# Attention stage: up products into the score ring, a DMA exchange for the rotary half, one exponential per quad, and the key's head mask on VectorE

## What is computed

```python
xn = layernorm(x)                                     # 32 sequences, T = 256, D = 128
q, k = l2norm(xn @ Wq), l2norm(xn @ Wk)               # 16 heads of 8
v = xn @ Wv
clock = softplus(xn @ clock_w + clock_b)              # one value per head
q, k = rope(q), rope(k)
gcp = exp(clip(cumsum(-softplus(xn @ gate_w + gate_b)), -60, 50))
q, k = q * gcp, k / (gcp + 1e-8)
p_exp = exp(p - max_t p) * clock                      # p = xn @ p_w + p_b
q, k = q / (cumsum(p_exp) + 1e-8), k * p_exp
out = softmax(causal(q @ k.T) / sqrt(8)) @ v
x1 = out @ out_w + out_b + residual
x2 = x1 + gelu(layernorm(x1) @ mlp_w1 + mlp_b1) @ mlp_w2 + mlp_b2
def rope(x): x1, x2 = even and odd elements of a head; return x1*cos - x2*sin, x1*sin + x2*cos
```

## Time and profile before

| | us |
|---|---|
| three runs, median | 2212.62 (2210.34 to 2213.51) |
| profiled execution, first to last instruction | 2164.4 |
| median less that span | 48.2 |
| one full step of the attention stage | 41.83 |
| full steps | 13 |
| first write of the expert layer's index table | about 769 |

### The profile page before, as it was taken

One profiled execution on the slowest core, in us unless ns is written; L12 is line 12 of the kernel. 1 busy time (PEld: TensorE's weight loads), 2 busy tenths in 40 slices (PEclk: granted clock), 3 DMA queues, 4 the chain that ended last, 5 costly groups with the idle time before them and its releaser, 6 DMA issues. The chain is left out here.

```text
span 2164.4 us, 37241 instructions
## 1 busy us (share of the span) xinstructions
PE 1849.2 (85%) x12576; PEld 954.5 (44%) x12600; DVE 1703.8 (79%) x3547; ACT 1474.7 (68%) x2917; POOL 1165.1 (54%) x720
## 2 busy tenths in 40 slices
PE   6999999999998459957889889898898988659996
PEld 2566666656665259952222222222222222124453
DVE  7778868877863437854899999999999998976776
ACT  5888888888885138845656666666666666437775
POOL 2122232242221027871789999999999998840001
PEclk9999999999999669977899999999999998879998
DMA  4100010011001012221100111001111100023333
GB/s 169 36 26 26 28 49 26 26 36 41 21 25 33 20 50 77 88 72 42 30 25 27 34 35 34 27 30 30 31 35 35 35 31 30 21 67 90 97 84 78
DMA packets 103708, 97.35 MB, mean 45 GB/s; under 512 B 9137, under 2 KB 86113, under 8 KB 103137
## 3 DMA queue, kind: packets, MB, share of 16 engines
q1 hardware_dynamic: 95584, 75.34, 12.4%
q0 software_dynamic: 6784, 18.10, 2.5%
q10 hardware_dynamic: 1152, 1.54, 0.2%
HBM read 45.87 MB, written 28.10 MB: 34 GB/s over the span
## 5 line engine op out<-in xcount | busy, mean ns | idle before, releaser
L1935 POOL TENSOR_TENSOR hc<-h,c_rep 128x1024 f32<-128x1024 f32 x256 | 627.8, 2463 | 137.9 <-DVE h L1899 136.7
L1899 DVE TENSOR_TENSOR_SCAN h<-decay,bank 128x1024 f32<-128x1024 f32 x241 | 551.0, 2286 | 22.5 <-issue 0.9
L1757 ACT ACTIVATE decay<-bank,neg_a_r 128x510 f32<-128x510 f32 x512 | 322.6, 683 | 257.5 <-PE bank L1634 257.1
L1618 PE MATMUL bank<-u_in,sel_rows 32*128 32x512 f32 x964 | 287.9, 675 | 95.7 <-DVE h L1899 95.6
L1634 PE MATMUL bank<-delta,sel_rows 32*128 32x512 f32 x1024 | 338.8, 677 | 0.9 <-ACT decay L1757 0.9
L1886 DVE TENSOR_TENSOR bank<-bank,b_rep 128x1024 f32<-128x1024 f32 x241 | 291.2, 1208 | 34.8 <-PE bank L1618 33.0
L992 POOL DMA_INDIRECT rows_in_dram<-row,idx x64 | 63.3, 989 | 318.3 <-DVE row L965 303.7
L574 ACT ACTIVATE es<-bank 128x384 f32<-128x384 f32 x512 | 208.9, 499 | 22.1 <-PE bank L373 21.8
L1618 PEld LDWEIGHTS bank<-u_in,sel_rows 32*128 32x128 f32 x964 | 76.0, 191 | 276.7 <-DVE h L1899 199.7
L1649 PE MATMUL bank<-hc,y_sel 128*32 128x512 f32 x1024 | 149.6, 660 | 0.8 <-POOL hc L1935 0.8
L1656 PE MATMUL bank<-xpad,w_conv 128*128 128x512 f32 x256 | 133.0, 634 | 3.2 <-ACT xc L1819 1.6
(11 more groups left out here) (341 smaller groups left out, 4170.0 us busy)
## 6 DMA issues: line engine op xcount, KB each, us to landing
r_tw<-r_o_t SPq DMA_DIRECT2D x96, 128.0 KB, 2.3
xvs<-xv SPq DMA_DIRECT2D x16, 512.0 KB, 2.9
u_wide<-u_rep_dram SPq DMA_DIRECT2D x30, 256.0 KB, 3.5
xs<-rows_in_dram SPq DMA_DIRECT2D x72, 68.0 KB, 1.8
front<-in_x_dram SPq DMA_DIRECT2D x16, 256.0 KB, 2.9
w<-in_w_dram SPq DMA_DIRECT2D x2, 2048.0 KB
xlb_dram<-front SPq DMA_DIRECT2D x16, 256.0 KB, 2.3
xlb_m<-xlb_dram SPq DMA_DIRECT2D x16, 256.0 KB
```

What stands on the lines that cost most here:

```text
L1618: last = pe.matmul(BD[n % 2][:, i * STEP:(i + 1) * STEP], sel[at:at + 32, r, :], u_in[p if n < NS else q][at:at + 32, hf, :], start=True, ...
L1757: act.activation(decay[n % 4][:, i, :, 1:], seq(DL[i])[:, :, 1:], ACT.Exp, scale=c["neg_a_r"][:, hf, g:g + 1]).then_inc(s["n_da"], 1)
L1899: dve.tensor_tensor_scan(flat(h[n % RING]), decay[n % 4].rearrange("p i b t -> p (i b t)"), flat(drive_0) if by_pool else BD[n % 2], 0.0, ...
L1935: pool.tensor_tensor(hc[n % RING][:, :, :], h[n % RING][:, :, :], c_rep[p if n < NS else q][:, :].unsqueeze(1).to_broadcast([P, 2, STEP]), ...
```

## The change

Five things change, all in the attention stage:

1. **Up products.** `up(0)` to `up(3)` write into the four banks of the ring, one after another, between `exps(5)` and `quad(6)`; the four gelus read them there. `quad(6)` waits for the last gelu. The down products are split: two token tiles ahead of `quad(7)`, two behind `weigh(6)`.
2. **Exchange.** The projections with `w_qs` and `w_ks` are gone. VectorE multiplies the one product with `cos` and with `sin`; two DMAs of 64 partitions each copy `rot_b` to `rot_s` with even and odd partitions exchanged (`swap`), and VectorE subtracts. That is four DMAs a step on SyncE's queue. The first product with `ones_blk` (L481) now waits for `rot_b` of q, and its place is ahead of `quad(0)`; the weights' load shrinks and is split in three.
3. **Merged exponentials.** `exps(n)` is one ScalarE instruction of 128x1536 over the four banks; `s_score` counts once a quad, at the last mask.
4. **The key's mask.** VectorE's last product with `pexp` is made four times, each with the mask as its scalar, at the start of the next step, between `pre[1]` and `pmax`; L953 and ScalarE's four copies are gone.
5. **Order.** On TensorE `back(3)` moves behind `quad(1)`, `weigh(7)` behind `quad(0)`, `quad(2)` ahead of `weigh(1)`, and the second product with `ones_blk` and the routing's product stand behind `back(0)`. On ScalarE `av_copy(3)` moves behind `exps(0)` and `exps(2)` ahead of `av_copy(0)`. GpSimd's L985 waits for `m_xl2` as well. `of` and `before` of the table's code move into `log`, to make room in SBUF.

```diff
+        def swap(sp, sem):
+            for to in range(2):
+                sp.dma_start(rot_s[to:P:2, :], rot_b[1 - to:P:2, :]).then_inc(sem, 16)
...
+                sp.wait_ge(s["f_rb"], one_on)
+                swap(sp, s["f_qsw"])
+                sp.wait_ge(s["f_kb"], one_on)
+                sp.wait_ge(s["f_rq"], one_on)
+                swap(sp, s["f_ksw"])
...
-                    pe.matmul(diag, c["ident_b"][:, :], c["mask_b"][:, :, :], start=False, stop=True,
-                              skip_group_check=True).then_inc(s["s_score"], 1)
+                    last = pe.matmul(diag, c["ident_b"][:, :], c["mask_b"][:, :, :], start=False, stop=True, skip_group_check=True)
+                last.then_inc(s["s_score"], 1)
...
             if tail:
                 pe.wait_ge(s["m_ht_sb"], k - 2)
-                up(0)
+                pe.wait_ge(s["s_exp"], 8 * (k - 2) + 6 if late else 8 * PAIRS)
+                for n in range(FC):
+                    up(n)
...
             if late:
+                if tail:
+                    pe.wait_ge(s["m_gelu"], 4 * k - 8)
                 quad(6, k - 2, p)
...
             if tail:
                 pe.wait_ge(s["m_gelu"], 4 * k - 8)
-                for j in range(TS):
...
+                down(range(0, 2))
             if late:
                 quad(7, k - 2, p)
-            if front:
-                pe.wait_ge(s["f_pe"], k + 1)
-                project(FB, c["w_qs"], s["f_qs"])
-            if late:
                 weigh(6, k - 2, p)
-                weigh(7, k - 2, p)
+            if tail:
+                down(range(2, TS))
+            if front:
+                pe.wait_ge(s["f_sq"], k + 1)
+                pe.wait_ge(s["f_rb"], k + 1)
+                pe.matmul(FA[:, :], c["ones_blk"], square[:, :], start=True, stop=True).then_inc(s["f_ssq"], 1)
...
             def exps(n, u):
-                for st in range(HS):
-                    act.wait_ge(s["s_score"], u * 32 + HS * n + st + 1)
-                    if st == 0:
-                        since(act, s["s_av"], u * 8 + n - 1)
-                    last = act.activation(es[(n % 2) * HS + st][:, :], RING[st][:, 0:3 * P], ACT.Exp, scale=DH ** -0.5)
-                last.then_inc(s["s_exp"], 1)
+                act.wait_ge(s["s_score"], u * 8 + n + 1)
+                since(act, s["s_av"], u * 8 + n - 1)
+                act.activation(es[n % 2][:, :, :], ring[:, :, 0:3 * P], ACT.Exp, scale=DH ** -0.5).then_inc(s["s_exp"], 1)
...
             if scores:
                 exps(0, k - 1)
+            if late:
+                av_copy(3, k - 2)
...
             if scores:
+                exps(2, k - 1)
                 av_copy(0, k - 1)
-                exps(2, k - 1)
...
-            if front:
-                act.wait_ge(s["f_k2"], k + 1)
-                since(act, s["s_score"], 32 * k - 32)
-                for v in range(HS):
-                    last = act.activation(k_m[p][:, v, :], rot_k[:, :], ACT.Copy, scale=c["head_mask"][:, v:v + 1])
-                last.then_inc(s["f_km"], 1)
...
+            if scores:
+                dve.wait_ge(s["f_k1"], k)
+                since(dve, s["s_score"], 8 * k - 16)
+                for v in range(HS):
+                    last = dve.scalar_tensor_tensor(k_m[q][:, v, :], rot_k[:, :], c["head_mask"][:, v:v + 1], pexp[:, :], ALU.mult, ALU.mult)
+                last.then_inc(s["f_k2"], 1)
...
+                dve.wait_ge(s["f_ra"], k + 1)
+                dve.wait_ge(s["f_qsw"], 32 * k + 32)
+                dve.tensor_tensor(rot[:, :], rot[:, :], rot_s[:, :], ALU.subtract).then_inc(s["f_rq"], 1)
...
                 pool.wait_ge(s["f_back"], k + 1)
+                if tail:
+                    pool.wait_ge(s["m_xl2"], k - 2)
                 pool.tensor_tensor(mag[:, 1, :], mag[:, 1, :], one_up[:, :], ALU.subtract).then_inc(s["f_lost"], 1)
```

More of the change, by code:

```diff
@@ L275, in attention @@
         end = sb("end", [1, E])
-        of = sb("of", [1, ETILES])
-        before = sb("before", [1, ETILES])
+        of, before = (log[0:1, 0, n * ETILES:(n + 1) * ETILES] for n in range(2))
         hi = sb("p_hi", [E * FC, P], bf16)
@@ L476, in pe_step @@
             if late:
-                back(3, k - 2)
+                weigh(7, k - 2, p)
             if front:
-                pe.wait_ge(s["f_sq"], k + 1)
-                pe.wait_ge(s["f_ra"], k + 1)
-                pe.matmul(FA[:, :], c["ones_blk"], square[:, :], start=True, stop=True).then_inc(s["f_ssq"], 1)
-                pe.wait_ge(s["f_rb"], k + 1)
+                pe.wait_ge(s["f_pe"], k + 1)
                 project(FB, c["w_k"], s["f_k"])
@@ L490, in pe_step @@
                 quad(1, k - 1, q)
-            if front:
-                pe.wait_ge(s["f_mq"], k + 1)
-                project(FA, c["w_ks"], s["f_ks"])
+            if late:
+                back(3, k - 2)
             if scores:
                 weigh(0, k - 1, q)
+            if scores:
+                quad(2, k - 1, q)
+                weigh(1, k - 1, q)
             if tail:
@@ L500, in pe_step @@
                 transposes(M, xl2, s["m_x2t"])
-            if scores:
-                weigh(1, k - 1, q)
-                quad(2, k - 1, q)
-            if tail:
-                pe.wait_ge(s["m_x2t_sb"], k - 2)
-                for j in range(TS):
-                    last = pe.matmul(M[:, j * E:(j + 1) * E], o_t[:, j * P:(j + 1) * P], c["cent"][:, :], start=True, stop=True)
-                last.then_inc(s["m_aff"], 1)
             if scores:
@@ L516, in pe_step @@
             if front:
-                pe.wait_ge(s["f_ka"], k + 1)
+                pe.wait_ge(s["f_kb"], k + 1)
                 pe.wait_ge(s["f_sk"], k + 1)
                 pe.matmul(FB[:, :], c["ones_blk"], square[:, :], start=True, stop=True).then_inc(s["f_ssk"], 1)
+            if tail:
+                pe.wait_ge(s["m_x2t_sb"], k - 2)
+                for j in range(TS):
+                    last = pe.matmul(M[:, j * E:(j + 1) * E], o_t[:, j * P:(j + 1) * P], c["cent"][:, :], start=True, stop=True)
+                last.then_inc(s["m_aff"], 1)
             if scores:
@@ L528, in pe_step @@
                 transposes(M, o_tok[p], s["m_ot"])
+            if scores:
+                weigh(2, k - 1, q)
+                quad(4, k - 1, q)
             if tail:
@@ L541, in pe_step @@
                 last.then_inc(s["r_rank"], 1)
-            if scores:
-                weigh(2, k - 1, q)
-                quad(4, k - 1, q)
             if mid:
@@ L593, in act_step @@
                 act.activation(v_a[q][:, :, :, 0:DH], FA.rearrange("p (j h d) -> p j h d", j=TS, h=H), ACT.Copy).then_inc(s["f_vaug"], 1)
-            if tail:
-                since(act, s["m_dn"], k - 3)
-                gelu(0)
             if late:
@@ L599, in act_step @@
             if tail:
-                gelu(1)
+                since(act, s["m_dn"], 2 * k - 6)
+                for n in range(FC):
+                    gelu(n)
             if front:
@@ L896, in dve_step @@
                 dve.tensor_reduce(first[:, :], hot_f[:, :, :], AX.X, ALU.max).then_inc(s["r_dve"], 1)
-            if scores:
-                heads_o(0, k - 1, q)
             if tail:
```

145 lines of the change are left out of this document (66 added, 79 removed).

## The result

The changed kernel takes 2299.55 us, median of 4 runs (2294.78 to 2304.22), against 2212.77 of the kernel before: a ratio of 1.040, 95% interval 1.037 to 1.042. It is slower by 87 us. The forecast was 2299.

What follows compares the result with a forecast made beforehand. The prediction took the chain of exponentials to bound the kernel: 13 full steps +86, first steps +8, last steps -7, sum +87 on the median 2212.6, so 2299 us; range 2240 to 2345.

Steps and rivals of the forecast that it cites:

- walk along the exponentials: Followed the eight exponentials through one full step, cutting its 41.83 us into four stretches and pricing each.
- What bounds it: Full step: the chain of exponentials is the limit, as quads cannot overlap; not TensorE's work, though busy 39.88 of 41.83.
- The rival that TensorE's work is the limit: Full step falls by the two products gone, 1.8 us, 13 times; 2182 us in all; chance 0.13.
- Merged exponential: On ScalarE: 1536 columns take about 1.48 us, ending 0.15 later than the group of four; the chain gains nothing.
- S1: End of exponential 5 to start of exponential 0: from 21.73 to 24.3 us, +2.5.
- S2: Start of exponential 0 to start of exponential 1: from 3.57 to 6.0 us, +2.4.
- S3: Start of exponential 1 to start of exponential 3: from 8.90 to 10.3 us, +1.4.
- First and last steps: Steps 0 to 2 lose 8 us (3 to 12); steps 16 to 18 gain 7 (3 to 10).
- No wait on `rot_s`: Sign in the changed profile: the exchange DMAs, 2.3 us each, land before rot_s is asked for, so cost nothing.
- The full clock in steps 3 to 15: Sign in the changed profile: the clock stays full throughout these steps.
- The rival that the clock falls: TensorE's 2 us gaps bring 1.2 GHz in the stretch from exponential 1 to 3: +3 a step, 2338 us; chance 0.10.
- my +6.6: Rise of one full step, from 41.83 to 48.4 us; 13 such steps give +86.

Runs made afterwards that it cites:

- ring_swap: ring_only plus the exchange: products with w_qs and w_ks gone, rot_s copied by DMA; 2163.1 us, 1.0005 of the kernel before.
- back3_first: Changed kernel with back(3) ahead of quad(1) and av_copy(3) ahead of exponential 0 again; 2251.5 us, 1.0196 of the kernel before.
- s3_order: back3_first with exponential 2 ahead of lgcp's, quad(3) ahead of back(0) and the products behind it, exponential 3 ahead of two logarithms; 2227.5 us, 1.0064.
- ring_only: Kernel before with only the up products moved into the score ring, gelus in a row, quad(6) behind; 2137.9 us, 0.9894.

## Why the prediction was right, and what in it was not

The time and the sign held, and so did the walk along the exponentials; one rival came true beside it. Step by step:

- **What bounds it**: right. The chain of exponentials explains each stretch, and TensorE's freed 1.8 us are worth nothing; `ring_swap` shows that by itself. The rival that TensorE's work is the limit is refuted.
- **Merged exponential**: 1.48 estimated, 1.444 measured (mean of 128).
- **S1**: 24.3 forecast, 24.67 measured, but from unlike rows. On the slower kind of chip before has 23.17, so the rise is 1.5 and not 2.5. Of its terms, `front` took 2.72 (3.0), the masks 3.20 (3.65 with the collision), and the wait of `weigh(6)` was 1.00 (2.0). These sizes were too large.
- **S2**: right in size (5.78 for 6.0) and in cause: `back3_first` takes it back to 3.3 with two moves.
- **S3**: 9.98 for 10.3, and `s3_order` shows that it is the order. L985 of before (now L981) does collide with the clip, at 1.32.
- **First and last steps**: against the kernel before profiled again, the changed kernel has lost 13.3 us when exponential 5 of step 2 ends (forecast 8), of them 7.8 up to exponential 0 of step 2 and 5.5 in the rest of that step, whose S3 takes 12.96 instead of 7.13 with the clock at half for part of it. From exponential 5 of step 15 on it gains 7.5 (forecast 7), and the 13 full steps between cost 87.3 (forecast 86). The cause that I gave for the first steps, a product with `ones_blk` that waits for the rotated q, stands in the trace (L482 waits 3.23 in step 0), and `ring_swap`, which has that wait but not the masks, loses 7.1 up to the same place; so the masks probably carry little of it. "No wait on `rot_s`" held: VectorE never waits for it in the changed kernel. These sums come to 93.1 and the two profiled spans differ by 97.8, while the medians differ by 87: the profiled execution was the slowest of the changed kernel's four.
- **"The full clock in steps 3 to 15"**: wrong. Every full step ran at half clock for 3.4 to 13.7 us, where neither profile of the kernel before has any in them. The rival that the clock falls, to which I gave 0.10, came true together with the main case, not instead of it: the clean step is +4.9, and the clock adds 1.6 on average. The Trainium skill, "TensorE: Matmul & The Clock Gate", section "HAM oscillation — how this bites in real kernels", says that gaps that come back in each pass bring the low clock back; here the traces agree only in part: the clock falls in all full steps of the changed kernel, but in two of 12 of `back3_first`, whose gaps also come back in each step, in three of 12 of `ring_swap` and in none of `ring_only`.

So the number came out because two errors cancel, which is luck. The rows of before lacked 1.43 a step that both kernels pay on the chips of the result, which makes +4.9 of my +6.6; and I left out a clock that costs about 1.6 to 2.

The accounting from the other side: `back(3)` took back 48 us, the order of S3 24 and `heads_o(2)` 13.6, together 35.5. That is 83.5 of 87.

Left open: how the clock's price depends on the length and place of the gaps, and whether the masks on VectorE would gain in an order of their own. The merged exponential was not run alone.

## What to carry to other kernels

A part that saves work off the chain of waits is worth nothing, and the idle time that it leaves may cost the clock, as in three of 12 steps of `ring_swap`. When operations in in-order queues are rearranged to make room for a good idea, price each operation that something critical now stands behind: here one transposition group behind a quad cost more than the whole good idea brought. Try each part alone; one of four (the ups in the ring) gained 1.1% by itself; the exchange took that away again, the masks cost 0.4 us a step, and the order cost the most.

## What the runs showed of the hardware

- The chips differ by 2.3% on the same program (2212 and 2162 us). On the slower kind ScalarE and VectorE are both released late by TensorE at the seam of two steps. The kernel profiled again shows it (compare, where the first up product starts 0.73 behind the copies; here it starts 2.16 behind them):

```profile
443.22 2.54 ACT L719 ACTIVATE k_m<-rot_k,consts 128x512 f32<-128x512 f32 x4
...
444.75 0.66 PE L352 MATMUL bank<-consts,h_tok 128*128 128x128 f32 x4
...
447.09 0.78 ACT L589 ACTIVATE h_t<-bank,vec 128x512 f32<-128x512 f32 x1 [1.33 <-remote]
447.13 0.75 DVE L776 TENSOR_SCALAR pre<-bank,vec 128x512 f32<-128x512 f32 x1 [1.32 <-PE bank L348]
```

  The transposes' record ends at 445.41 and `h_t` starts 1.7 later; in the profile of the quick kind it is 0.27. The cause was not found.
- VectorE and GpSimd stretch each other where both work on SBUF alone: four masked products took 2.73 without a GpSimd operation (at 46.18 in the changed kernel's trace), 3.20 beside one and 4.75 beside several; the clip took 1.32 beside L981 and 0.41 without a GpSimd operation. GpSimd's L981 itself took 2.05 instead of 1.27. An operation of VectorE that reads a bank was not stretched: L862 took 0.68 beside GpSimd's L983 in each of steps 3 to 14. The Trainium skill, "SBUF — State Buffer", section "Who interferes with whom", describes this as an exclusive lock on a shared pair of ports; the traces agree.
- The four-bank exponential of 1536 columns takes 1.44 us, less than the 1.62 to 1.64 of four separate ones. By the walk it gains nothing on the chain, as it waits for all four masks; no run shows it alone.
